# Experts' network of a MetaFormer kernel: row groups of 32 in the first products, column tiles in the second

## The reference, cut to what matters

```python
logits = jnp.einsum('bsd,ed->bse', x, gate_w) + gate_b
probs = jax.nn.softmax(logits, axis=1)
vals, idx = jax.lax.top_k(probs.transpose(0, 2, 1), K)
...
pooled = jnp.einsum('bked,bke->bed', gathered, topv)
h = jnp.concatenate([pooled.transpose(1, 0, 2), ones], axis=-1)
h = jax.nn.gelu(jnp.einsum('ebd,edh->ebh', h, weight1), approximate=False)
h = jnp.concatenate([h, ones], axis=-1)
out = jnp.einsum('ebh,eho->ebo', h, weight2)
...
outputs = outputs.at[jnp.arange(Bn)[:, None], flat_idx].add(weighted)
```

## Time and profile before

| | |
|---|---|
| median of 3 runs | 586.11 us (584.59 to 586.77) |
| profiled execution | 586.52 us, of which span 584.5 |
| PE busy | 545.3 us, 93% of the span |
| DVE, ACT, POOL busy | 329.1, 290.4, 115.1 us |
| TensorE's mean granted clock | 0.962 of full |
| largest line on the chain | L741, the recurrent sweeps, 39% |

### The profile page before, as it was taken

The page is one execution under the profiler, slowest core; times in us unless marked ns, Lnnn a source line. Parts: engine busy times, 40 slices in busy tenths (PEclk is TensorE's granted clock), DMA queues, the critical chain, the costliest instruction groups (busy, mean ns, idle before and its releaser), DMA issues.

```text
span 584.5 us, 22848 instructions
## 1 busy us (share of the span) xinstructions
PE 545.3 (93%) x9964; PEld 485.4 (83%) x9964; DVE 329.1 (56%) x802; ACT 290.4 (50%) x814; POOL 115.1 (20%) x240
## 2 busy tenths in 40 slices
PE   8979899999998999978999999969999999986997
PEld 7979889999997885767888888869988888986862
DVE  2747767644436936773545454535555455569726
ACT  4556665543358502455444444424445777567600
POOL 4000000000025000002333333653331033371000
PEclk9999999999999789999999999979999999996969
DMA  9930774070000000000000022420000244500007
GB/s 347 369 144 2 289 290 148 1 288 1 1 2 2 1 22 1 1 1 2 4 4 4 4 65 72 115 49 4 4 3 4 40 83 77 101 2 1 2 2 287
DMA packets 50250, 41.54 MB, mean 71 GB/s; under 512 B 44998, under 2 KB 45126, under 8 KB 48934
## 3 DMA queue, kind: packets, MB, share of 16 engines
q1 hardware_dynamic: 49304, 38.51, 20.4%
q0 software_dynamic: 704, 1.18, 0.9%
q10 hardware_dynamic: 144, 0.39, 0.2%
HBM read 27.49 MB, written 4.19 MB: 54 GB/s over the span
## 4 chain that ended last, share of the span: by engine, by line
PE 78%; DVE 10%; POOL 4%; ACT 4%; issue 2%; DMA 1%; SPq 1%; POOLq 0%; DVEq 0%; ACTq 0%
PE PS L741 39%; PE PS L709 5%; PE PS L533 5%; PE PS L479 3%; PE PS L608 2%; PE PS L578 2%; PE PS L557 2%; PE PS L517 2%; PE PS L564 2%; PE PS L458 2%; POOL RCD L398 2%; POOL RE L395 2%; PE PS L638 2%; PE PS L488 2%; PE PS L437 1%
## 5 line engine op out<-in xcount | busy, mean ns | idle before, releaser
L741 PE MATMUL PS<-RE,conv_sb 128*64 128x64 f32 x6048 | 230.0, 227 | 5.4 <-DVE RE L1117 3.9
L741 PEld LDWEIGHTS PS<-RE,conv_sb 128*64 128x64 f32 x6048 | 202.2, 138 | 33.2 <-DVE RE L1117 4.6
L867 ACT COPY PS<-convb_sb 128x64 f32<-128x64 f32 x504 | 108.2, 215 | 112.7 <-DVE RE L1129 80.7
L1129 DVE SCALAR_TENSOR_TENSOR RE<-PS,RCD 128x64 f32<-128x64 f32 x252 | 56.6, 224 | 57.1 <-PE PS L741 40.4
L407 POOL COPY RCD<-RE 128x128 f32<-128x128 f32 x126 | 37.0, 294 | 151.2 <-DVE RE L1129 151.1
L1129 DVE SCALAR_TENSOR_TENSOR RE<-PS,RE 128x64 f32<-128x64 f32 x126 | 32.4, 258 | 29.6 <-PE PS L741 21.5
L1129 DVE SCALAR_TENSOR_TENSOR RE<-PS,RB 128x64 f32<-128x64 f32 x126 | 28.3, 224 | 28.2 <-PE PS L741 19.6
L479 PE MATMUL PS<-warm 128*128 128x128 bf16 x448 | 37.1, 256 | 3.8 <-DVE warm L894 1.4
L479 PEld LDWEIGHTS PS<-warm 128*128 128x128 bf16 x448 | 34.4, 118 | 4.9 <-ACT RB L844 1.6
L395 POOL TENSOR_TENSOR RE<-RA 128x1024 f32<-128x1024 f32 x3 | 5.7, 1892 | 161.8 <-ACT RA L837 161.8
L533 PE MATMUL PS<-RE,RB 128*64 128x64 f32 x1024 | 32.1, 223 | 2.9 <-issue 2.4
(11 more groups left out here) (115 smaller groups left out, 758.4 us busy)
## 6 DMA issues: line engine op xcount, KB each, us to landing
RE<-wspec SPq DMA_DIRECT2D x8, 2048.0 KB, 8.7
RA<-x_in SPq DMA_DIRECT2D x8, 512.0 KB, 7.8
RCD<-x_in SPq DMA_DIRECT2D x1, 4096.0 KB, 13.6
out<-RA SPq DMA_DIRECT2D x8, 512.0 KB, 2.7
RCD<-RB SPq DMA_DIRECT2D x58, 64.0 KB, 2.6
RE<-RCD SPq DMA_DIRECT2D x32, 80.0 KB, 2.3
conv_sb<-conv_w SPq DMA_DIRECT2D x1, 768.0 KB, 19.7
w_sb<-w SPq DMA_DIRECT2D x2, 264.0 KB
```

The lines of the kernel that those rows point to most:

```text
L741: m = pe.matmul(conv_bank(s, u, c)[o:o + OC], conv_sb[:, s, d, o:o + OC], prev, start=False, stop=(d == 2), skip_group_check=True)
L867: act.copy(banks_of, convb_sb[:, s:s + 1].unsqueeze(2).to_broadcast([P, c1 - c0, n])).then_inc(s_seed, 1)
L1129: dve.scalar_tensor_tensor(out=state[:, state_slot(s, u), b0:b1, 1:1 + HO], in0=conv_bank(s, u, c), scalar=0.0, in1=row_at(SRC[s], s, q, u ...
```

## The change

Four experts now stand beside each other on the partitions, each in a row group of 32. The means are turned by eight small products (`mean` as weights, picked columns of the identity moving) straight into that layout, and copied by one instruction. The first bias no longer is a 33rd row: four products `b1` x `pick` write it into banks 0, 1, 6 and 7 before the last pooling group, one bank per row group, and the first products accumulate on it. They run over four experts' row groups and two halves of hidden units before they come back to a tile. Gelu reads two banks at a time, in two instructions. The second products write four partition groups in turn. VectorE adds the second bias in four pieces, each into its own block of the zeroed `eout` (128 rows now), and a product with `fold` (four identities on top of each other) takes the place of the transpose back. The warming products are 4 (new, behind pooling), 4, 6, 8 and 8.

```diff
+ER, EC = P // C, NE * C // P
...
-        w1_sb = sb("w1_sb", [C + 1, NE, NHID])
-        w2_sb, b2_sb = sb("w2_sb", [P, 2, NE, C]), sb("b2_sb", [C, 2, NE])
+        w1_sb = sb("w1_sb", [P, EC, NHID])
+        b1_sb, pick_sb = sb("b1_sb", [NE, 2, NHID]), sb("pick_sb", [NE, ER, EC * B])
+        w2_sb, b2_sb = sb("w2_sb", [P, 2, NE, C]), sb("b2_sb", [P, 2, EC])
+        fold_sb = sb("fold_sb", [P, C])
...
-        N_SET, N_PAR = 4, 7
+        N_SET, N_PAR = 4, 10
...
+        def hid_bank(r):
+
+            return r if r < 2 else r + 4
...
-                         (w2_sb, w2), (b2_sb, b2), (own_sb, own)):
+                         (b1_sb, b1), (pick_sb, pick), (w2_sb, w2), (b2_sb, b2), (fold_sb, fold), (own_sb, own)):
...
+                for r in range(ER):
+                    pe.matmul(PS[:, hid_bank(r), 0:EC * B], b1_sb[:, l, :], pick_sb[:, r, :], start=True, stop=False,
+                              skip_group_check=True)
                 pool_tokens(3).then_inc(s_pl, 1)
+                keep_warm(2, 4)
                 pe.wait_ge(s_mean, l + 1)
-                pe.transpose(PS[0:MO, 5, 0:P], mean[:, :], ident).then_inc(s_pt, 1)
-                keep_warm(3, 6)
+                own_cols = ident.rearrange("p (j q r e) -> p q r j e", q=2, r=ER, e=EC)
+                for q in range(2):
+                    for r in range(ER):
+                        m = pe.matmul(PS[C * r:C * r + C, 5, 16 * q:16 * q + 16], mean[:, C * q:C * q + C],
+                                      own_cols[:, q, r], start=True, stop=True)
+                m.then_inc(s_pt, 1)
+                keep_warm(2, 4)
...
-                for e in range(NE):
+                for e in range(EC):
                     for a in range(2):
                         units = slice(MO * a, MO * (a + 1))
-                        m = pe.matmul(PS[units, 6, B * e:B * e + B], w1_sb[:, e, units], pooled[:, :, e],
-                                      start=True, stop=True)
+                        for r in range(ER):
+                            rows = slice(C * r, C * r + C)
+                            m = pe.matmul(PS[units, hid_bank(r), B * e:B * e + B], w1_sb[rows, e, units],
+                                          pooled[rows, e, :], start=False, stop=True, skip_group_check=True)
                 m.then_inc(s_h, 1)
-                keep_warm(3, 8)
+                keep_warm(2, 6)
                 pe.wait_ge(s_g, l + 1)
-                for e in range(NE):
-                    m = pe.matmul(PS[0:C, 7, B * e:B * e + B], w2_sb[:, l, e, :], hid[:, e, :], start=True, stop=True)
+                for e in range(EC):
+                    for r in range(ER):
+                        m = pe.matmul(PS[C * r:C * r + C, 4, B * e:B * e + B], w2_sb[:, l, EC * r + e, :],
+                                      hid[:, EC * r + e, :], start=True, stop=True)
                 m.then_inc(s_o, 1)
-                keep_warm(3, 8)
+                keep_warm(2, 8)
                 pe.wait_ge(s_ob, l + 1)
-                pe.transpose(PS[:, 4, 0:C], eout[:, :, :].rearrange("p b e -> p (b e)"),
-                             ident[0:C, 0:C]).then_inc(s_ot, 1)
-                keep_warm(3, 10)
+                pe.matmul(PS[:, 5, 0:C], eout[:, :, :].rearrange("p b e -> p (b e)"), fold_sb[:, :],
+                          start=True, stop=True).then_inc(s_ot, 1)
+                keep_warm(2, 8)
...
-                act.activation(hid[:, :, :].rearrange("p e b -> p (e b)"), PS[:, 6, 0:P], ACT.Gelu).then_inc(s_g, 1)
+                for r in (0, 2):
+                    m = act.activation(hid[:, EC * r:EC * r + 2 * EC, :].rearrange("p (y e) b -> p y (e b)", y=2),
+                                       PS[:, hid_bank(r):hid_bank(r) + 2, 0:EC * B], ACT.Gelu)
+                m.then_inc(s_g, 1)
...
-            dve.memset(pooled[C:C + 1, :, :], 1.0).then_inc(s_set, 1)
+            dve.memset(eout[:, :, :], 0.0).then_inc(s_set, 1)
...
-                for q in range(2):
-                    m = dve.tensor_copy(pooled[0:C, q:B:2, :],
-                                        PS[C * q:C * q + C, 5, 0:P].rearrange("p (j q e) -> p q j e", q=2, e=NE)[:, q])
-                m.then_inc(s_pc, 1)
+                dve.tensor_copy(pooled[:, :, :].rearrange("p e (j q) -> p e j q", q=2),
+                                PS[:, 5, 0:EC * B].rearrange("p (q j e) -> p e j q", q=2, e=EC)).then_inc(s_pc, 1)
                 dve.wait_ge(s_o, l + 1)
-                dve.tensor_tensor(eout[:, :, :].rearrange("p b e -> p e b"),
-                                  PS[0:C, 7, 0:P].rearrange("p (e b) -> p e b", b=B),
-                                  b2_sb[:, l, :].unsqueeze(2).to_broadcast([C, NE, B]), ALU.add).then_inc(s_ob, 1)
+                for r in range(ER):
+                    rows = slice(C * r, C * r + C)
+                    m = dve.tensor_tensor(eout[rows, :, EC * r:EC * r + EC],
+                                          PS[rows, 4, 0:EC * B].rearrange("p (e b) -> p b e", b=B),
+                                          b2_sb[rows, l, :].unsqueeze(1).to_broadcast([C, B, EC]), ALU.add)
+                m.then_inc(s_ob, 1)
```

More of the change, by code:

```diff
@@ L38, with build_kernel @@
 AX_X = mybir.AxisListType.X
-def build_kernel(nc, x_in, dft, wspec, conv_w, conv_b, gate_w, gate_b, w1, w2, b2, own, out):
+def build_kernel(nc, x_in, dft, wspec, conv_w, conv_b, gate_w, gate_b, w1, b1, pick, w2, b2, fold, own, out):
     with ExitStack() as ctx:
@@ L75, in build_kernel @@
         mean = sb("mean", [P, MO])
-        pooled = sb("pooled", [C + 1, B, NE])
+        pooled = sb("pooled", [P, EC, B])
         hid = sb("hid", [P, NE, B])
-        eout = sb("eout", [C, B, NE])
+        eout = sb("eout", [P, B, NE])
         espread = sb("espread", [P, B, C])
@@ L1083, in experts @@
                 dve.wait_ge(s_pt, l + 1)
-                for q in range(2):
-                    m = dve.tensor_copy(pooled[0:C, q:B:2, :],
-                                        PS[C * q:C * q + C, 5, 0:P].rearrange("p (j q e) -> p q j e", q=2, e=NE)[:, q])
-                m.then_inc(s_pc, 1)
+                dve.tensor_copy(pooled[:, :, :].rearrange("p e (j q) -> p e j q", q=2),
+                                PS[:, 5, 0:EC * B].rearrange("p (q j e) -> p e j q", q=2, e=EC)).then_inc(s_pc, 1)
                 dve.wait_ge(s_o, l + 1)
-                dve.tensor_tensor(eout[:, :, :].rearrange("p b e -> p e b"),
-                                  PS[0:C, 7, 0:P].rearrange("p (e b) -> p e b", b=B),
-                                  b2_sb[:, l, :].unsqueeze(2).to_broadcast([C, NE, B]), ALU.add).then_inc(s_ob, 1)
+                for r in range(ER):
[4 more added lines that the diff above has]
+                m.then_inc(s_ob, 1)
                 dve.wait_ge(s_ot, l + 1)
                 dve.scalar_tensor_tensor(out=espread[:, :, :],
-                                         in0=PS[:, 4, 0:C].unsqueeze(1).to_broadcast([P, B, C]),
+                                         in0=PS[:, 5, 0:C].unsqueeze(1).to_broadcast([P, B, C]),
                                          scalar=rsum[:, :], in1=own_sb[:, :].unsqueeze(2).to_broadcast([P, B, C]),
@@ L1191 @@
     gate_b = np.stack([np.tile(a[f"L{l}_ffn_gate_b"], B) for l in range(2)], 1)
-    w1 = np.stack([a[f"L{l}_ffn_weight1"].transpose(1, 0, 2) for l in range(2)])
+    w1 = np.stack([a[f"L{l}_ffn_weight1"][:, :C].reshape(ER, EC, C, NHID).transpose(0, 2, 1, 3).reshape(P, EC, NHID)
+                   for l in range(2)])
+    b1 = np.stack([a[f"L{l}_ffn_weight1"][:, C] for l in range(2)], 1)
+    pick = np.repeat(np.eye(NE, dtype=np.float32), B, 1).reshape(NE, ER, EC * B)
     w2 = np.stack([a[f"L{l}_ffn_weight2"][:, :NHID].transpose(1, 0, 2) for l in range(2)], 1)
-    b2 = np.stack([a[f"L{l}_ffn_weight2"][:, NHID].T for l in range(2)], 1)
+    b2 = np.stack([a[f"L{l}_ffn_weight2"][:, NHID].reshape(ER, EC, C).transpose(0, 2, 1).reshape(P, EC) for l in range(2)], 1)
+    fold = np.tile(np.eye(C, dtype=np.float32), (ER, 1))
     own = np.repeat(np.eye(B, dtype=np.float32), NE, 0)
     arrays = {"x_in": x, "dft": dft_tables(), "wspec": ws, "conv_w": conv_w, "conv_b": conv_b,
-              "gate_w": gate.reshape(P, 2, BL * NE), "gate_b": gate_b, "w1": w1, "w2": w2, "b2": b2, "own": own}
+              "gate_w": gate.reshape(P, 2, BL * NE), "gate_b": gate_b, "w1": w1, "b1": b1, "pick": pick,
+              "w2": w2, "b2": b2, "fold": fold, "own": own}
     arrays = {k: np.ascontiguousarray(v) for k, v in arrays.items()}
```

## The result

The changed kernel takes 578.02 us (median of four runs, 575.70 to 578.40), against 586.44 (four runs, 584.59 to 588.56) for the kernel before on the same chip: ratio 0.985, interval 0.980 to 0.990. The forecast of 582.3 had the sign right, and its range ended at 580.3: the kernel gained about 4 us more than was forecast. The profiled execution took 578.05 us, of which span 576.2; TensorE's mean granted clock was 0.982, where it had been 0.962.

A forecast was written before the change was run, and what follows sets the result against it. The prediction took TensorE's own sequence and its handovers (78% of the chain) as the bound. Terms of -2.4 us in block 0 and -2.85 in block 1, with +1.0 for the clock, took 586.52 to 582.3 us; range 580.3 to 585.6.

The forecast's parts named there:

- What the clock takes back: Scatters, starting 5.25 us earlier in all, run at half rate until the clock rises: +1.0 us given back.
- Gelu: Activation after the first products: two instructions for one, still covered, with two fewer warm-ups: -0.25 us a block.
- Second products: Experts' second products over four column tiles: 14 ns apart instead of 54, -1.25 us a block (bound -1.0).
- Fold and spread: Fold product replacing the transpose back, two warm-ups fewer, then the spread before the scatter: net 0 a block.
- First products: Experts' first products over eight tiles: 7 ns apart instead of 30, -1.45 us in block 0, -1.9 in block 1.
- Bias in PSUM: Four bias matmuls before the last pooling group, on the path: +0.6 us a block (bounds +0.3 and +0.9).
- Turning the means: One transpose becomes 16 instructions and two copies become one, before the first products: net -0.15 us a block.
- bias add: VectorE's second bias in four instructions instead of one, just fitting under the warm-ups' cover: +0.1 us a block.
- Row groups that don't overlap: Rival, chance 0.20: first products keep their 30 ns; 585.1 us.
- stand in each other's way: Rival, chance 0.07: row tiles' loads wait for products in other row groups, first products get slower; 590.9 us.
- The clock rise stays put: Rival, chance 0.15: the rise keeps its moment, so half the 5.25 us goes back at half rate; 583.9 us.

The follow-up runs named there:

- experiments 3 and 5: The kernel before with the changed kernel's warm-up places and numbers (586.50 us); the kernel before with `pooled` laid out as channel, expert, image (585.82 us).
- experiment 4: The kernel before with more warm-ups (10 behind the pooling, then 10, 14, 14, 10), old products untouched: 583.19 us.
- first step of experiment 7: The changed kernel with two of a block's four bias products moved behind the first group's weight transposes, replacing 7 of 14 warm-ups: 579.93 us.
- experiment 6: The changed kernel with each second product made four times, to the same result: 584.65 us.
- second step of experiment 7: The changed kernel with two bias products behind the first weight transposes and two behind the last pooling group, replacing warm-ups at both places: 580.84 us.
- experiment 1: The changed kernel with row groups in turn (576.73 us), column tiles in turn (578.14 us), or both (581.48 us).

## Why the prediction was right in sign and too small

**What failed: "What the clock takes back".** It asked only when the rise would come after the fall, and took for given that the fall near 213.6 and 558.3 stays; of 5.25 us it let 1.0 go back. No term let the clock add to the gain, so that the range ended at 580.3 where all of the 5.25 is kept. But the same shortening that it had summed also shortens the stretch that brought the clock down, while the warm-ups in it stay nearly as many. With no fall there is nothing to give back, and what the old kernel had lost comes on top: its scatters ran at half rate for 1.6 and 3.9 us, half of which is 0.8 and 1.95, and -0.75 and -1.87 were measured. The old kernel with more warm-ups shows this gain by itself (3.7 us in the medians), the changed kernel without warm-ups shows its loss (6.9). The thirteen profiles agree: between first product and scatter's end the clock falls in both blocks of the three that have the old products and the old number of warm-ups or two less (experiments 3 and 5 and the kernel before) and of the changed kernel without warm-ups; in neither block of the changed kernel, of the one with the old places and of the old products with more warm-ups; in one block or none of the other variants of the changed kernel. How short the stage must be for how many warm-ups no run says.

**The same error inside the stage** made the terms too small behind the first products. "Gelu", "Second products" and "Fold and spread" were worked out at the half clock; at full clock the eight warm-ups that covered Gelu in 0.97 us take about 0.6 (L486 x8 above), and the steps came out 0.2, 0.15 and 0.3 larger a block than forecast. Gelu, which the forecast kept covered with 0.19 us to spare, is not: the weight loads of L711 wait 0.16 us for it.

**First products**: the mechanism held, four row groups work side by side. The spacing is 10 ns, not the 7 of eight tiles at 57 ns, so -1.28 and -1.66 for -1.45 and -1.9 (in block 1 a stop of 0.10 us is in it). The Trainium skill's rule in TensorEngine Tiling (Array Packing), Key Properties, that tiles load and multiply in parallel, agrees with the 10 ns against 20 in turn. But the reason for the old 30 ns, "a tile costs some 57 ns a product", was wrong in general: one row group over two column halves has 20, 40 a tile, and the 54 ns of the second products were at the half clock.

**Second products**: a quarter by tiles as forecast, but of the 32 ns that one tile has at full clock (experiment 4), not of the 54 at half: 8 ns, not 14. The bound "-1.0, twice that spacing" was miscounted: 31 x 0.028 = 0.87 for 1.68 is -0.8. The sum doesn't use it.

**Bias in PSUM**: +0.64 against +0.6, and it is the one large cost. Its eight instructions and the change to pooling take 1.00 us from start to start (211.04 to 212.04), four of them 0.56 in the first step of experiment 7, so one is 0.11 as taken, and 0.12 remain, where the forecast had 0.17 for the change of shape. The same section of the Trainium skill says that a change of tiling mode drains the array; the 0.12 agrees so far, but no run shows what it consists of. **Turning the means** (-0.20 for -0.15) and **bias add** (four in 0.79, as taken; -0.02 for +0.1) were right, and the cover of the bias add is used up: TensorE now waits 0.37 us for L1112.

**The rivals.** Row groups that don't overlap, or stand in each other's way: the 10 ns exclude both, and with row groups in turn, at 20 ns and not the first rival's 30, the kernel was no slower than now (576.73 us). "The clock rise stays put" shared the error: it assumed a fall. A rival without one was missing; with the forecast's own terms it would have given 586.52 - 5.25 - 0.8 - 1.95 = 578.5. That this comes so near to 578.05 is in part luck: the steps gave 6.52 and not 5.25, and +0.67 elsewhere hides about half of the difference.

## What to carry to other kernels

Before asking how much of a gain a low clock gives back, ask whether the shortened stretch still brings the clock down, and price both: no fall returns the lost half of every stretch at half rate, which here was more than the products' own gain (5.9 of 9.1 us by the profiles, experiment 4). Read the granted clock against the warm-ups that stay: even where most of them have left the chain they may be worth much (6.9 us here). A row saved in a stage, as the bias's here, can be lost again to the clock or to a stop, so compare the mean granted clock of several runs along with the times, and the rows beside the one that was moved.

## What the runs showed of the hardware beyond that

- Products of 33 rows come 29 ns apart over two column halves, products of 32 rows 20, and over four row groups and two halves 10; with 32-column weights of 128 rows it is 54 ns in one tile at the half clock, 32 at full (experiment 4), 23 where the tile changes after every eight instructions, and 8 where it changes after every two.
- In long runs of products 8 to 10 ns apart TensorE sometimes stops for "issue": 1.79 us behind 94 instructions (experiment 6), and in the second step of experiment 7, in its timeline, 0.37 behind 47:

```profile
211.61 0.67 PE L709 MATMUL PS<-pooled,w_sb 32*64 32x8 f32 x47
212.65 0.34 PE L709 MATMUL PS<-pooled,w_sb 32*64 32x8 f32 x17 [0.37 <-issue]
```

The records point to the fetching of TensorE's own instructions. The first and second products of the changed kernel and its variants have nine stops in which two starts lie over 100 ns apart. Whatever product stands there, they come behind the same few places of the list of matmul instructions, counted from the start of the run: behind number 2750 or 2878 in block 0, and 9913 or 10041 in block 1, each pair 128 apart (256 instructions with the weight loads). And each ends 2.2 to 2.8 us after the latest packet, of 16 KB, began on queue q8, which the pages call "instruction"; in the page of experiment 6 (queue, kind, packets, MB, share of 16 engines):

```profile
q8 instruction: 82, 1.34, 1.0%
```

Where the products there come 20 ns apart or more, as in experiment 1's rows in turn, they pass these places 2.6 us or more after that and show no such stop. No run varied the fetching itself, so the cause is argued and not shown.
